# Written step orders for the binarised feed-forward stage and the first steps of layer 3, on three engines

## What is computed

```python
def _quantize_activations_groupwise(x):
    n = x.shape[0]
    gs = n // NUM_GROUPS                     # 5 groups of 3 images
    ...
        ag = x[g * gs:(g + 1) * gs]
        gamma = jnp.max(jnp.abs(ag))
        xq = xq.at[g * gs:(g + 1) * gs].set(jnp.clip(ag * QB / (gamma + EPS), -QB + EPS, QB - EPS))
def _bitlinear(x, W, b):
    Wb = _binarize_weights_groupwise(W)
    y = jnp.einsum('btc,oc->bto', x, Wb) + b
    return _quantize_activations_groupwise(y)
h = _bitlinear(x, W1, b1)                    # 96 -> 384
h = jax.nn.gelu(h, approximate=False)
out = _bitlinear(h, W2, b2)                  # 384 -> 96
...
t = t + _L2_ffn_ref(_ln_t(t), ...)
t = t + _L3_attn_ref(_ln_t(t), ...)
```

## Time and profile before

| | us |
|---|---|
| median of 3 runs (812.35 to 813.57) | 813.28 |
| the profiled execution, its own time | 818.12 |
| its span, first to last instruction | 815.9 |
| PE busy | 749.0 |
| DVE busy | 581.7 |
| ACT busy | 569.0 |
| POOL busy | 252.4 |

### The profile page before, as it was taken

One profiled execution on the slowest core, in us unless ns is written; L12 is line 12 of the kernel. 1 busy time (PEld: TensorE's weight loads), 2 busy tenths in 40 slices (PEclk: granted clock), 3 DMA queues, 4 the chain that ended last, 5 costly groups with the idle time before them and its releaser, 6 DMA issues.

```text
span 815.9 us, 16956 instructions
## 1 busy us (share of the span) xinstructions
PE 749.0 (92%) x5265; PEld 585.4 (72%) x5265; DVE 581.7 (71%) x1430; ACT 569.0 (70%) x1419; POOL 252.4 (31%) x485
## 2 busy tenths in 40 slices
PE   1896999999999879999998985899999999999997
PEld 1874787778887767777775673677777797677775
DVE  6247776767677556888884997588888735877775
ACT  2324787787777657888885835588888738777875
POOL 1902346556653350212121000031221110544334
PEclk9998999999999989999999988799999959999999
DMA  6000000111011132333320001233233103123220
GB/s 214 1 1 0 1 12 13 18 22 16 15 21 21 25 83 79 100 94 91 101 78 1 0 2 51 66 89 105 80 104 86 41 1 81 49 49 78 68 49 20
DMA packets 60073, 41.36 MB, mean 51 GB/s; under 512 B 33904, under 2 KB 52464, under 8 KB 59888
## 3 DMA queue, kind: packets, MB, share of 16 engines
q1 hardware_dynamic: 60016, 40.63, 19.5%
HBM read 12.24 MB, written 3.21 MB: 19 GB/s over the span
## 4 chain that ended last, share of the span: by engine, by line
PE 77%; DVE 12%; ACT 3%; issue 3%; DMA 2%; SPq 1%; POOL 1%; POOLq 0%; DVEq 0%; ACTq 0%
PE ps L1253 11%; PE ps L992 10%; PE ps L1403 8%; PE ps L1418 8%; PE ps L1093 6%; PE ps L997 5%; PE ps L1021 3%; PE ps L1077 3%; PE ps L1035 3%; PE ps L1000 2%; PE ps L1022 2%; PE ps L942 2%; PE ps L1065 2%; DMA qk<-hl 1%; PE ps L1173 1%
## 5 line engine op out<-in xcount | busy, mean ns | idle before, releaser
L622 ACT ACTIVATE ee<-ps,nmax 128x128 f32<-128x128 f32 (+1 forms) x576 | 204.8, 444 | 13.2 <-DVE nmax L1592 6.4
L1253 PE MATMUL ps<-w,ee 128*128 128x128 f32 x960 | 134.7, 273 | 1.9 <-ACT big L609 1.7
L1253 PEld LDWEIGHTS ps<-w,ee 128*128 128x128 f32 x960 | 112.7, 142 | 13.5 <-ACT ee L622 2.6
L609 ACT ACTIVATE big<-ps 128x512 f32<-128x512 f32 (+1 forms) x192 | 96.4, 554 | 24.9 <-PE ps L1253 23.1
L1595 DVE TENSOR_REDUCE nmax<-ps 128x2 f32<-128x256 f32 x192 | 97.4, 549 | 14.6 <-PE ps L1000 10.0
L1716 DVE TENSOR_TENSOR hhl<-ee,hhl 128x512 fp32r<-128x512 f32 x96 | 79.1, 829 | 32.7 <-ACT hhl L861 31.1
L992 PE MATMUL ps<-kh,big 128*128 128x256 f32 x384 | 94.4, 390 | 1.5 <-POOL big L382 1.2
L1592 DVE TENSOR_REDUCE nmax<-ps 128x4 f32<-128x1024 f32 x48 | 58.7, 1223 | 44.7 <-PE ps L992 44.6
L1403 PE MATMUL ps<-qk,w1hl 128*128 128x512 f32 x288 | 84.9, 404 | 0.0
L1418 PE MATMUL ps<-hhl,w2hl 128*96 128x512 f32 x288 | 82.3, 396 | 2.2 <-DVE big L1945 1.9
L526 POOL TENSOR_TENSOR xc<-big,xc 96x512 f32<-96x512 f32 x32 | 52.0, 1626 | 99.6 <-DVE big L1945 99.0
(11 more groups left out here) (261 smaller groups left out, 1339.2 us busy)
## 6 DMA issues: line engine op xcount, KB each, us to landing
qk<-hl SPq DMA_DIRECT2D x256, 96.0 KB, 3.1
big<-moe_gate SPq DMA_DIRECT2D x8, 768.0 KB, 6.8
w<-w_in SPq DMA_DIRECT2D x1, 1735.0 KB, 13.1
xc<-x_in SPq DMA_DIRECT2D x4, 384.0 KB, 5.8
l_mix<-on SPq DMA_DIRECT2D x32, 48.0 KB, 2.1
tok<-l_mix SPq DMA_DIRECT2D x16, 96.0 KB, 2.0
out<-xc SPq DMA_DIRECT2D x8, 192.0 KB, 2.1
w<-w_in SPq DMA_DIRECT2D x1, 998.0 KB, 9.5
```

The costliest lines, as they stand in the source:

```text
L609: nc.scalar.activation(et[:, h, 0:w], ps[:, 4 + hh, 0:w], ACT.Copy).then_inc(own(l, f"et{hh}"), 1)
L622: last = nc.scalar.activation(ee[:, ke, hh, qc, 0:w], src, ACT.Exp, bias=nmax[:, kp, hh, qc:qc + 1])
L1253: last = nc.tensor.transpose(ps[:, 4 + hh, b * P:(b + 1) * P], ee[:, u, hh, qc, tc * P:(tc + 1) * P], ident)
```

## The change

- `F2_PE` has all first-layer steps ahead of the second layer, and takes in the steps T, Q (projection), S (score unit) and V (value projection) of layer 3 that stood behind the stage.
- `F2_ACT` takes in L (load of the table for Ln and Exp), R, N, C, Q (`queries`) and X (`exps`); the gelu table is loaded ahead of the first copy.
- `F2_DVE` has q0 right behind a0, a1 and a2 ahead of q1, and brings f, b, k, y nearer to each other; n3 is gone and b3 has come, so group 3 is normalised on ACT.
- The second layer uses three pairs of banks (`Y2_BANKS`) and waits for the group two before; the transposes use banks 4 and 5 throughout.
- q has four small operations, of which the first two don't wait for each other, f has two.

```diff
-F2_PE = ["h0", "h1", "h2", "h3", "y0", "h4", "y1", "y2", "y3", "y4"]
...
+F2_PE = ["h0", "h1", "h2", "h3", "h4", "y0", "y1", "y2", "y3", "T0", "Q0", "y4", "T1", "Q1", "S0", "T2", "S1", "T3", "V0", "T4"]
...
+Y2_BANKS = [(6, 7), (0, 1), (6, 2), (0, 1), (6, 2)]
...
-        bound = sb("bound", [P, NG])
+        bound = sb("bound", [P, 2, NG])
...
-            return 6 if b == 0 else 7 if g == 0 else 5
+            return Y2_BANKS[g][b]
...
-            return (3 if g < NG - 1 else 4) + b, lo + b * half, half
+            return 4 + b, lo + b * half, half
...
+                    nc.scalar.preload_act_table_set("gelu_and_others")
                     for step in F2_ACT:
...
+                        elif step[0] == "R":
+                            ln3_root(g)
+                        elif step[0] == "N":
+                            ln3_norm(g)
+                        elif step[0] == "C":
+                            ln3_channels(g)
+                        elif step[0] == "Q":
+                            queries(3, g, g)
+                        elif step[0] == "X":
+                            exps(3, 0, 0, 0)
...
-                if g < 3:
+                if g < NG - 1:
                     pe.wait_ge(sg("ln3_normed_act"), g + 1)
...
+                        elif step[0] == "T":
+                            ln3_transposes(g)
+                        elif step[0] == "Q":
+                            if g == 0:
+                                pe.wait_ge(sg("l3_wq"), 4)
+                                pe.wait_ge(sg("f2_y2"), 2)
+                            else:
+                                parts_ready(3, 0)
+                            project_qk(3, g, g)
+                        elif step[0] == "S":
+                            if g == 0:
+                                keys_ready(3, 0, 0, 0)
+                            pe.wait_ge(sg("f2_y2"), 2 * g + 8)
+                            score_unit(3, 0, g, g, g)
+                        elif step[0] == "V":
+                            parts_ready(3, 1)
+                            project_v(3, 0, 0)
...
-                                if g >= 1:
-                                    pe.wait_ge(sg("f2_y2"), 2 * (g - 1) + b + 1)
+                                if g >= 2:
+                                    pe.wait_ge(sg("f2_y2"), 2 * (g - 2) + b + 1)
...
-                        link(V.tensor_scalar(m, m, QEPS, None, ALU.add))
-                        link(V.reciprocal(q, m))
-                        link(V.tensor_scalar(q, q, QB, None, ALU.mult))
+                        last = V.tensor_scalar(q, m, QEPS, 1.0 / QB, ALU.add, ALU.mult)
+                        if k == 0:
+                            V.tensor_scalar(bound[:, 0, g:g + 1], m, QEPS, (QB - QEPS) / QB, ALU.add, ALU.mult)
+                            last = V.tensor_scalar(bound[:, 1, g:g + 1], m, QEPS, -(QB - QEPS) / QB, ALU.add, ALU.mult)
+                        link(last)
+                        link(V.reciprocal(q, q))
...
-                            top, low = amax[:, 1, g:g + 1], bound[:, g:g + 1]
-                            link(V.tensor_scalar(top, top, (QB - QEPS) / QB, None, ALU.mult))
-                            link(V.tensor_scalar(low, top, -1.0, None, ALU.mult))
+                            top, low = bound[:, 0, g:g + 1], bound[:, 1, g:g + 1]
```

More of the change, by code:

```diff
@@ L87 @@
 RES_BANK = [1, 1, 2, 3, 2, 1, 2, 3]
-F2_PE = ["h0", "h1", "h2", "h3", "y0", "h4", "y1", "y2", "y3", "y4"]
-F2_ACT = ["c0", "c1", "c2", "e0", "c3", "e1", "c4", "e2", "e3", "e4"]
-F2_DVE = ["a0", "a1", "q0", "a2", "q1", "a3", "q2", "y0", "a4", "q3", "y1", "f0", "q4", "y2", "f1", "y3", "b0", "f2", "b1", "y4", "b2", "f3", "k0", "f4", "k1", "n3", "m0", "n4", "m1", "v0"]
+F2_PE = ["h0", "h1", "h2", "h3", "h4", "y0", "y1", "y2", "y3", "T0", "Q0", "y4", "T1", "Q1", "S0", "T2", "S1", "T3", "V0", "T4"]
+F2_ACT = ["c0", "c1", "c2", "e0", "c3", "c4", "e1", "e2", "e3", "e4", "L0", "R0", "N0", "R1", "C0", "N1", "Q0", "R2", "N2", "C1", "Q1", "R3", "N3",
+          "C2", "R4", "X0", "C3", "C4"]
+F2_DVE = ["a0", "q0", "a1", "a2", "q1", "q2", "a3", "a4", "q3", "y0", "q4", "f0", "y1", "b0", "f1", "y2", "b1", "f2", "k0", "y3", "b2", "f3", "y4",
+          "k1", "b3", "m0", "f4", "n4", "m1", "v0"]
+Y2_BANKS = [(6, 7), (0, 1), (6, 2), (0, 1), (6, 2)]
 C96, N96 = columns(W96)
@@ L746, in _ @@
                     norm_root("gn1b", C, *GROUP["gn1b"])
[L747 to L763, removed]
                 def unit(j, k, i):
@@ L845, in _ @@
                                                          ACT.Copy).then_inc(sg("f2_y1"), 1)
+                        elif step[0] == "L":
+                            nc.scalar.preload_act_table_set("natural_log_exp_and_others")
+                        elif step[0] == "R":
[8 more added lines that the diff above has]
+                            exps(3, 0, 0, 0)
                         else:
@@ L887, in ln3_transposes @@
             def ln3_transposes(g):
-                if g < 3:
+                if g < NG - 1:
                     pe.wait_ge(sg("ln3_normed_act"), g + 1)
                 else:
-                    pe.wait_ge(sg("ln3_normed_dve"), g - 2)
+                    pe.wait_ge(sg("ln3_normed_dve"), 1)
                 for b in range(2):
@@ L895, in ln3_transposes @@
                     if g >= 1:
-                        pe.wait_ge(sg("l3_xn"), 2 * g - 1 + b if g < NG - 1 else 2 * g)
+                        pe.wait_ge(sg("l3_xn"), 2 * g - 1 + b)
                     for t in range(n):
@@ L1182, in _ @@
                 if l == 3:
[L1183 to L1197, removed]
                     pe.wait_ge(sg("f2_y2"), 2 * NG)
```

## The result

The changed kernel takes **804.01 us** (four runs, 802.23 to 806.04), the kernel before beside it 812.82: a ratio of 0.9887 [0.9858, 0.9915], 8.8 us less. 802.1 had been forecast, with a range of 799.8 to 805.5. Its profiled execution took 806.04 (forecast 806.9).

What follows compares the result with a forecast made beforehand. VectorE was taken to bound the stage, its chain running mostly there. The stage's 10.4 us less plus the tail's 0.8 made 11.2, taking the median from 813.28 to 802.1 us, range 799.8 to 805.5 (forecast's own 799.8 to 804.5).

Steps and rivals of the forecast that it cites:

- The stage by its sum: From first absmax's end to last token group's normalisation: VectorE work 50.2 plus waits, 53.5 us instead of 63.8.
- The chains: Scale steps q and f on VectorE: fewer linked small operations save 3.0 us, all on the chain.
- The all-reduces: GpSimd's all-reduces, exposed ahead of q0, f1, f2, f3: VectorE waits 4 x 0.65 = 2.6 us.
- the rival of a longer all-reduce: GpSimd's all-reduce outlasts its row by 0 to 2.1 us: 807.7 at 1.3, 812.5 at 2.1; chance 0.08.
- n3: Normalisation of group 3 moves from VectorE to ScalarE: VectorE's work falls 1.4 us net, ScalarE's price zero.
- The load of the gelu table: On ScalarE ahead of the first copies, while TensorE finishes layer 2: costs zero, at most 1.28 us.
- m0: VectorE step after layer 3's first score unit: 0 to 0.5 us lost waiting, taken as 0.
- k0 and the clock: Before VectorE's k0: no slack; y3 takes 5.86 us on TensorE, and the query copy is just in time.
- the rival of k0 and the clock: TensorE stays at 1.2 GHz from y3 to T4: k0 some 3 us late, 5 of 11.2 lost, 806.9; chance 0.08.
- an idle piece of more than 1 us at k0: Sign in the profile after: none was expected ahead of k0; one would point to the clock or ScalarE.
- The tail: After the last normalisation: the value projection moves ahead of transposes T4, into TensorE's wait, 0.8 us less.
- Nothing comes of it: Rival: layer 3's first units wait for something this stage does not set, such as transfers; 813, chance 0.03.

Runs made afterwards that it cites:

- the repeats: The changed kernel and the kernel before, each run once more unaltered: 804.59 us against 814.72, ratio 0.9879 [0.9851, 0.9907].
- both runs: New scale chains alone in the kernel before: 811.63 us, ratio 0.9981; old scale chains put back in the changed kernel: 807.24 us, ratio to before 0.9917.
- the repeat: The changed kernel once more, with no edit: 804.59 us (six runs), ratio to the kernel before 0.9879.

## Why the prediction was right

**The stage by its sum.** n4 was to end 53.5 after a0, and ended 53.39 after it; to the weighing 11.2 were to go, and 11.23 did (69.36 to 58.13). With the repeats it is 10.2 to 11.2, so the hit to 0.1 is in part luck of the two profiles.

**The chains** (3.0): right, by both runs, 3.0 alone and 3.07 of VectorE's work undone. q's head is 0.51 (450.66 to 451.17; forecast 0.52). The sum by the rule in the Trainium skill (VectorE: DVE Perf Modes, The DRAIN you can't avoid), that leaving semaphores out saves nothing, was 1.2 less in all. The trace does not agree with that rule for these operations of 128x1: three without a link start 0.06 to 0.07 apart, the linked ones 0.18 to 0.20.

**The all-reduces** (2.6 of waiting): the right places, too large by 0.8; VectorE waited 0.55 + 3 x 0.41 = 1.78. GpSimd starts 0.10 after y1's absmax ends (478.28 to 478.38), near the 0.14 that the forecast had, but the hop back, taken at the same size, is 0.03 (478.73 to 478.76); and b's 0.08 lies under three of the four, which the forecast had not taken off. R4's wait is 0.61 instead of 0.74. The rule in the Trainium skill (Perfetto Trace Analysis, GPSIMD Engine Instruction) that such spans are unreliable stood beside the rival of a longer all-reduce. At the four exposed places the row holds, as the doubled all-reduce shows; beside a clip it read 1.17 instead of 0.35.

**n3** (1.4): done on ScalarE in time, since n4 waits for R4 alone; but undone it cost only 0.60, for the reason that follows. The load of the gelu table ahead of the first copies cost nothing, as forecast: from layer 2's last projection to a0 stand 4.58 before (443.31 to 447.89) and after (442.98 to 447.56). Nor does any wait of VectorE name the other load.

**m0** (0, at most 0.5): the one term outside its bound. From k0's start to S0 passed 7.42 and to m0 8.84, near the forecast's 7.2 and 8.7, but above what it called "an upper bound". But VectorE, sooner by the 0.8 that the all-reduces had not cost, came to m0 0.69 too soon. The two misses cancel, which the forecast could not know, but for a reason: the way over y3, the copies and SP's transfers starts with y1's first addition and has a length of its own, so what VectorE saves between that addition and m0 is waited off there. What it saves ahead of y1 counts in full: with the old chains y3 began 2.41 later after a0 (29.58 instead of 27.17), and from there to S0 passed 17.48, against 17.47 in the changed kernel. The forecast's sentence that the chain runs on VectorE through the stage is wrong for 477.28 to 496.17.

**k0 and the clock:** the forecast (y3 5.86, just in time) is the profile of the changed kernel; the rival is the repeat, in part. y3 took 7.48, and 1.24 was waited at k0, not 3 as the rival had it, since the clock was back at 2.4 GHz for T0 and y4 (4.15). With it the repeat shows an idle piece of more than 1 us at k0, which the forecast had named as a sign of being wrong. TensorE idled 2.79 ahead of y3 where 1.6 had been forecast: y0, y1 and y2 were through at 474.48 instead of 476.1.

**The tail** (0.8): n4's end to the weighing took 5.53 before and 4.73 now, 0.80 less. In the second profiles the same piece took 4.35 and 4.03, only 0.32 less, so the agreement to 0.01 is luck: the piece changes with the execution by more than the term, and the clock differed too (granted 0.50 from 515 to 519 in the first profile of before, 0.63 from 513 to 517 in the second). "Nothing comes of it" falls all the same, since layer 3's first units followed the stage at once.

**The time.** The profiled execution was to take 806.9 and took 806.04. The medians differ by 8.8 and 10.1 instead of 11.2, which both intervals contain (11.2 less is 0.9862 of 813.28). The step with the weakest ground was to take the whole of a stage's gain off a median of three runs, since single executions differ by some 4 us outside the stage. Whether the true gain is nearer 10 than 11 stays open. Two figures do not come out of the prediction's own terms: the range's 804.5 (with m0's 0.5 and the table's 1.3 it is 803.9) and the 806.9 of the rival of k0 and the clock (with 5 of 11.2 gone it is 807.1). Nothing in the account hangs on either.

## What to carry to other kernels

When a list is reordered to take out waits, find the second-longest way through the same stage, here matmul, copy, transfers, scores; what is saved between the point where it branches off and the point where the two meet counts only until the other way is the longer one. Buffers and orders are one change: each brought about 2 us alone here, and together with the chains 3.6 more than the sum of the parts (2.1 to 5.0, depending on the profiles compared). To judge such a stage, measure between two events of the trace rather than by the span, whose other parts differ more between executions than most single edits bring.

## What was not expected of the hardware

- The way from GpSimd back to VectorE adds almost nothing here: an all-reduce's row ends 0.03 before VectorE goes on (478.73 to 478.76), while GpSimd starts 0.10 to 0.14 after VectorE's absmax ends.
- An all-reduce of one column had a row of 0.35 to 0.38 wherever it stood clear of a clip, and of 1.17 in the three places where it ran beside one.
- The same 36 matmuls behind idle pieces of 2.79 and 2.80 took 5.86 and 7.48 in two executions of one kernel. With bank 3 for y3, and idle pieces of 0.69 and 1.26 around it, the granted clock read 1.00 from 476 to 482; behind the next piece, of 2.01, it read 0.78 from 482 to 484 and then 0.50 in one kernel, and in another with the same steps there 1.00 and then 0.56. The fall came in both, but not at the same time.
- Eight transfers of 96 KB that SP issues one behind the other: the first seven issues take 0.58 to 0.60 each, and the landing of the eighth takes 3.15 more. That makes 7.8 from the query copy's end (486.99) to S0, longer than y3 itself.
